# Joining the exit stage of a state space layer and the projection stage that follows it into one software pipeline

## The reference, cut to what matters

```python
y = y * rsqrt(mean(y*y) + 1e-5) * rms_w          # mamba2: gated output, root mean square norm
ym = y @ W_out + skip_scale * xs
ym = layernorm(ym, ln_w, ln_b)                   # over the 128 channels of a token
x = x + (ym @ proj_w + proj_b)
t = layernorm(x)                                 # over the channels, no weights
h = t @ W_gat                                    # 16 columns: 4 heads x 4 experts
a_src, a_dst = (h*att_src).sum(-1), (h*att_dst).sum(-1)      # 4 columns each
```

## Time and profile before

| | |
|---|---|
| median of 3 runs | 17695.13 us (17678.79 to 17721.8) |
| the profiled execution | 17696.22 us, its span 17694.7 us |
| `mamba_out` in the trace | from 11103 to about 11614 us |
| `heads`, second call | from about 11614 to 11976 us |
| busy share of the span | PE 41%, DVE 45%, ACT 25%, POOL 54% |

### The profile page before, as it was taken

How to read it: one execution, slowest core, us unless ns; L and a number is a source line. 1 busy time by engine, 2 the same in 40 slices (tenths; PEclk the granted TensorE clock), 3 DMA queues, 4 the chain that set the end, 5 groups by cost and what they waited for, 6 DMA issues and landing times. The chain is left out here.

```text
span 17694.7 us, 238235 instructions
## 1 busy us (share of the span) xinstructions
PE 7275.7 (41%) x86506; PEld 3912.4 (22%) x86506; DVE 7922.3 (45%) x12617; ACT 4414.1 (25%) x7103; POOL 9481.4 (54%) x10003
## 2 busy tenths in 40 slices
PE   0179711145221222136799999872112211222114
PEld 0123311023110111012355555331111111111012
DVE  9978576643111111175688888531111111111128
ACT  0123233322110011005665566641001110111000
POOL 0012477777777777660110000157777777777764
PEclk9589855577665666568899999986556655666556
DMA  1011221143222222244211111443222222222226
GB/s 47 0 50 44 72 52 21 20 114 113 61 61 55 54 61 62 57 156 131 60 49 48 46 48 49 154 119 65 58 55 58 61 58 55 58 61 61 53 55 224
DMA packets 949454, 1207.72 MB, mean 68 GB/s; under 512 B 371956, under 2 KB 587092, under 8 KB 929236
## 3 DMA queue, kind: packets, MB, share of 16 engines
q1 hardware_dynamic: 394036, 571.90, 9.9%
q0 software_dynamic: 328768, 179.97, 7.4%
q10 hardware_dynamic: 225888, 444.68, 7.4%
HBM read 672.45 MB, written 523.25 MB: 68 GB/s over the span
## 5 line engine op out<-in xcount | busy, mean ns | idle before, releaser
L1005 POOL DMA_INDIRECT g_got<-table,g_ring x8192 | 7740.1, 945 | 2520.4 <-issue 2490.9
L1203 DVE TENSOR_TENSOR g_z<-g_gs,g_wide 128x512 f32<-128x512 f32 x64 | 44.0, 688 | 5364.3 <-DMA g_gs<-rows 5364.3
L1046 PE MATMUL g_ffn<-g_xn,g_w 128*128 128x512 f32 x1024 | 556.9, 688 | 3967.1 <-ACT g_hid L1060 3940.4
L1046 PE MATMUL g0s_turn<-g_xn,g_w 128*128 128x512 f32 x1024 | 554.3, 685 | 2670.4 <-ACT g0s_ei L1060 2669.1
L1159 ACT ACTIVATE g_wide<-g_z 128x512 f32<-128x512 f32 x64 | 38.5, 601 | 6083.4 <-DVE g_z L1203 6083.4
L571 POOL DMA_INDIRECT m2b_got<-dst,k_blki x256 | 243.3, 950 | 2185.2 <-DVE m2b_le L583 2108.4
L1046 PEld LDWEIGHTS g_ffn<-g_xn,g_w 128*128 128x128 f32 x1024 | 190.4, 215 | 4287.6 <-ACT g_hid L1060 4193.6
L1046 PEld LDWEIGHTS g0s_turn<-g_xn,g_w 128*128 128x128 f32 x1024 | 189.7, 214 | 2988.8 <-ACT g0s_ei L1060 2921.7
L1338 POOL DMA_INDIRECT g_tot<-state,k_last_row x512 | 598.5, 1169 | 156.1 <-issue 156.1
L571 POOL DMA_INDIRECT cb_got<-dst,k_blki x256 | 250.6, 979 | 725.4 <-DVE cb_le L583 662.4
L951 POOL DMA_INDIRECT ad<-h_hs,k_start_row x512 | 504.5, 985 | 242.9 <-issue 147.7
(11 more groups left out here) (438 smaller groups left out, 19170.3 us busy)
## 6 DMA issues: line engine op xcount, KB each, us to landing
g_got<-table,g_ring POOLq DMA_INDIRECT x8192
ffn<-g_y ACTq DMA_DIRECT2D x128, 1024.0 KB
g_yin<-ffn SPq DMA_DIRECT2D x128, 1024.0 KB
rows<-g_got SPq DMA_DIRECT2D x512, 192.0 KB
g_gs<-rows ACTq DMA_DIRECT2D x64, 1536.0 KB, 6.4
state<-g_out ACTq DMA_DIRECT2D x64, 1536.0 KB, 5.5
h_x<-x SPq DMA_DIRECT2D x128, 256.0 KB
xn<-h_xn ACTq DMA_DIRECT2D x128, 256.0 KB
```

Of the source, the lines that this page charges most:

```text
L1005: pool.indirect_dma_start(self.got[:,par,k,:],None,self.table,bass.IndirectOffsetOnAxis(ap=self.ring[:,par,k:k+1].bitcast(u32),axis=0)).th ...
L1046: TE.matmul(self.hP[:,f,:],self.w1[:,e,f*P:f*P+P],self.xs[:,par,:],start=True,stop=True).then_inc(self.up,1)
```

## The change

The second call of `heads` goes, and its work becomes further sub-stages of `mamba_out`, on tiles that are still in SBUF: x3 is stored but not loaded again.

- PE gets `hn` mean (5), `hn` variance (6) and `table_rows` (7). Its order in a step is 6, 0, 5, 2, 3, 7, 4, 1.
- ACT gets `hn` square (6), `hn` root (7) and `leave` (8): a copy of the table rows out of PSUM, the store of xn, a second copy of the 16 a_dst columns into `adst`, and the store of the table rows. Its order is 7, 4, 1, 6, 3, 0, 8: the three roots, then the three squares, then `leave`. `root` has one Ln of 1024 columns in place of two of 512.
- DVE gets `hn` centre (5) and `hn` scale (6). Its order is 5, 2, 6, 3, 1, 4, 0.
- Both Norms share one variance bank, `vP`: nm's variance of tile i waits for hn's Ln of tile i-3, hn's variance of tile i for nm's Ln of tile i+2.
- `adst` has a place for each of the 64 tiles, so the scatters of POOL need no buffer back; POOL waits for them once at the end.
- Loading x and storing x3 move from POOL to SP, whose program is written out in full, without a loop: in step k y and xs of tile k, x of tile k-3, store of x3 of tile k-5.
- In every Norm of the program the logarithm is written over the squares (`self.log=self.sq`).

```diff
...
-    def __init__(self, nc, room, name, mean_w, eps, source, arrived, dest, dest_free):
+    def __init__(self, nc, room, name, mean_w, eps, source, arrived, dest, dest_free, var=None, var_free=None, mean=None):
...
-        self.log=room.sb(name+"_log",[P,2,T])
+        self.log=self.sq
...
-        self.mean=room.pb(name+"_mean",[P,T])
-        self.var=room.pb(name+"_var",[P,T])
+        self.mean=room.pb(name+"_mean",[P,T]) if mean is None else mean
+        self.var=room.pb(name+"_var",[P,T]) if var is None else var
+        self.var_free=var_free
...
+        if self.var_free: self.var_free(pe,i)
         self.nc.tensor.matmul(self.var[:,:],self.mean_w,self.sq[:,par,:],start=True,stop=True).then_inc(self.spread.sem,1)
...
         qP=r.pb("qP",[P,T])
+        vP=r.pb("vP",[P,T])
+        hp=r.pb("hp",[P,2,4,HW])
...
-        out=Stores(r,"out")
-        squared,meaned,logged,rooted,scaled,mixed,skipped,affine,projected,added=r.flags("squared meaned logged rooted scaled mixed skipped affine projected added")
-        nm=Norm(nc,r,"n",mw[:,:],eps[:,0:1],lambda i,par:ym[:,par,:],lambda e,i,par: skipped.of(e,i),lambda i,par:nn[:,par,:],lambda e,i,par: projected.before(e,i,2))
+        x_out_in,xn_stored,t_stored=r.pair("x_out"),r.pair("xn_out"),r.pair("t_out")
+        def stored(eng,sems,i,par):
+
+            if not (isinstance(i,int) and i<2): eng.wait_ge(sems[par],(i-par)*8)
+        sent=r.sem("sent")
+        picked=r.sem("picked")
+        send_gate=r.sem("send_gate")
+        squared,meaned,logged,rooted,scaled,mixed,skipped,affine,projected,added,rows,copied=r.flags("squared meaned logged rooted scaled mixed skipped affine projected added rows copied")
+        def rows_free(dve,i,par):
+            stored(dve,xn_stored,i,par)
+            rows.before(dve,i,2)
+        nm=Norm(nc,r,"n",mw[:,:],eps[:,0:1],lambda i,par:ym[:,par,:],lambda e,i,par: skipped.of(e,i),lambda i,par:nn[:,par,:],lambda e,i,par: projected.before(e,i,2),
+                vP[:,:],lambda e,i: hn.logged.of(e,i-3))
+        hn=Norm(nc,r,"hn",mw[:,:],eps[:,0:1],lambda i,par:xo[:,par,:],lambda e,i,par: added.of(e,i),lambda i,par:xn[:,par,:],rows_free,
+                vP[:,:],lambda e,i: nm.logged.of(e,min(i+2,TILES-1) if isinstance(i,int) else i+2))
...
+            for d,v in ((wos[:,:,:],wo),(rm[:,:],rms),(sk[:,:],skip.partition_broadcast(P)),(lw[:,:],lnw),(lb[:,:],lnb),(pws[:,:],pw),(pbs[:,:],pb),(sm[:,:],same_mean),(mw[:,:],ones),
+                        (w[:,0:16],wg),(at[:,:],att.partition_broadcast(P))):
+                sp.dma_start(d,v).then_inc(w_in,16)
+            def load(i):
+                scaled.before(sp,i,2)
+                sp.dma_start(yt[:,i%2,:,:],y.rearrange("q p n -> p q n")[:,:,i*T:(i+1)*T]).then_inc(y_in[i%2],16)
+                skipped.before(sp,i,2)
+                at_=i//TPI*PADT+i%TPI*T+2
+                sp.dma_start(xst[:,i%2,:],xs[:,at_:at_+T]).then_inc(s_in[i%2],16)
+            def load_x(i):
+                added.before(sp,i,2)
+                sp.dma_start(xt[:,i%2,:],x[:,i*T:(i+1)*T]).then_inc(x_in[i%2],16)
+            def store(i):
+                added.of(sp,i)
+                sp.dma_start(x_out[:,i*T:(i+1)*T],xo[:,i%2,:]).then_inc(x_out_in[i%2],16)
+            for k in range(TILES+5):
+                if k<TILES: load(k)
+                if 0<=k-3<TILES: load_x(k-3)
+                if k>=5: store(k-5)
+            for sems in (x_out_in,xn_stored,t_stored):
+                for v in sems: sp.wait_ge(v,TILES//2*16)
         @block.tensor
         def _(pe):
             nm.pe_start(pe)
-            for f in (meaned,mixed,projected): f.start(pe)
-            pe.wait_ge(w_in,16*9)
-            pe.wait_ge(ready,1)
+            hn.pe_start(pe)
+            for f in (meaned,mixed,projected,rows): f.start(pe)
+            pe.wait_ge(w_in,16*11)
+            pe.wait_ge(ready,3)
...
-            lagged(pe,TILES,[mean_square,mix,lambda i,p:nm.pe_mean(pe,i,p),lambda i,p:nm.pe_var(pe,i,p),project],last_first=True)
+            def table_rows(i,par):
+                hn.normed.of(pe,i)
+                copied.before(pe,i,1)
+                for q in range(4):
+                    last=nc.tensor.matmul(hp[:,par,q,:],xn[:,par,q*P:(q+1)*P],w[:,:],start=True,stop=True,skip_group_check=True)
+                last.then_inc(rows.sem,1)
+            lagged(pe,TILES,[mean_square,mix,lambda i,p:nm.pe_mean(pe,i,p),lambda i,p:nm.pe_var(pe,i,p),project,lambda i,p:hn.pe_mean(pe,i,p),lambda i,p:hn.pe_var(pe,i,p),table_rows],order=[6,0,5,2,3,7,4,1])
...
-                for q in range(2):
-                    last=nc.scalar.activation(rs[:,par,q,:],rP[:,q,:],ACT.Ln,bias=eps[:,0:1])
-                last.then_inc(logged.sem,1)
+                nc.scalar.activation(rs[:,par,:,:],rP[:,:,:],ACT.Ln,bias=eps[:,0:1]).then_inc(logged.sem,1)
                 logged.of(act,i)
                 nc.scalar.activation(rs[:,par,:,:],rs[:,par,:,:],ACT.Exp,scale=-0.5).then_inc(rooted.sem,1)
-            lagged(act,TILES,[square,root,lambda i,p:None,lambda i,p:nm.act_square(act,i,p),lambda i,p:nm.act_root(act,i,p)],last_first=True)
+            def leave(i,par):
+                rows.of(act,i)
+                stored(act,t_stored,i,par)
+                nc.scalar.copy(hs[:,par,:,:],hp[:,par,:,:]).then_inc(copied.sem,1)
+                nc.scalar.dma_start(xn_out[:,bass.ds(i*T,T)],xn[:,par,:]).then_inc(xn_stored[par],16)
+                copied.of(act,i)
+                nc.scalar.copy(adst[:,bass.ds(i,1),:,:].rearrange("p a q f -> p (a q) f"),hs[:,par,:,20:24]).then_inc(picked,1)
+                nc.scalar.dma_start(table[bass.ds(i*T,T),:].rearrange("(q p) f -> p q f",p=P),hs[:,par,:,:]).then_inc(t_stored[par],16)
+            lagged(act,TILES,[square,root,lambda i,p:None,lambda i,p:nm.act_square(act,i,p),lambda i,p:nm.act_root(act,i,p),lambda i,p:None,
+                              lambda i,p:hn.act_square(act,i,p),lambda i,p:hn.act_root(act,i,p),leave],order=[7,4,1,6,3,0,8])
...
+            for k in range(2):
+                nc.vector.tensor_tensor(prod[:,k,:],w[:,0:16],at[:,16*k:16*k+16],ALU.mult).then_inc(w_prod,1)
+            dve.wait_ge(w_prod,2)
+            for k in range(2):
+                nc.vector.tensor_reduce(w[:,16+4*k:20+4*k],prod[:,k,:].rearrange("p (h e) -> p h e",e=4),AX.X,ALU.add).then_inc(ready,1)
...
             def add_x(i,par):
                 projected.of(dve,i)
                 landed(dve,x_in,i,par)
-                out.done.before(dve,i,2)
+                stored(dve,x_out_in,i,par)
+                hn.centred.before(dve,i,2)
                 nc.vector.scalar_tensor_tensor(xo[:,par,:],qP[:,:],pbs[:,0:1],xt[:,par,:],ALU.add,ALU.add).then_inc(added.sem,1)
-            lagged(dve,TILES,[scale,add_skip,lambda i,p:nm.dve_centre(dve,i,p),norm,add_x],last_first=True)
+            lagged(dve,TILES,[scale,add_skip,lambda i,p:nm.dve_centre(dve,i,p),norm,add_x,lambda i,p:hn.dve_centre(dve,i,p),lambda i,p:hn.dve_scale(dve,i,p)],order=[5,2,6,3,1,4,0])
         @block.gpsimd
         def _(pool):
-            load(1,1)
-            with pool.Fori(0,TILES//2-1) as t:
-                for par in range(2):
-                    store(t*2+par,par)
-                    load(t*2+par+2,par)
-                    out.landed(pool,t*2+par,par)
...
+            for i in range(TILES):
+                pool.wait_ge(picked,i+1)
+                pool.sem_inc(send_gate,1)
+                for q in range(4):
+                    k=i*4+q
+                    pool.indirect_dma_start(ad,bass.IndirectOffsetOnAxis(ap=keep.start_row[:,k:k+1],axis=0),adst[:,i,q,:],None).then_inc(sent,16)
+            pool.wait_ge(sent,TILES*64)
...
-        mamba_out(nc,y,xs,x2,a["wo"],a["rms"],a["skip"],a["lnw"],a["lnb"],a["pw"],a["pb"],a["c_same_mean"],a["c_ones"],x3)
-        project(1,x3)
+        mamba_out(nc,y,xs,x2,a["wo"],a["rms"],a["skip"],a["lnw"],a["lnb"],a["pw"],a["pb"],a["c_same_mean"],a["c_ones"],x3,
+                  a["wg1"],a["att1"],xn,table,keep[1],ad[1])
         attend(1,x3,out)
```

More of the change, by code:

```diff
@@ L2083, with mamba_out @@
 PADT=TOK+2
-def mamba_out(nc, y, xs, x, wo, rms, skip, lnw, lnb, pw, pb, same_mean, ones, x_out, tag="m3"):
+def mamba_out(nc, y, xs, x, wo, rms, skip, lnw, lnb, pw, pb, same_mean, ones, x_out, wg, att, xn_out, table, keep, ad, tag="m3"):
     with ExitStack() as ctx:
@@ L2097, in mamba_out @@
         xo=r.sb("xo",[P,2,T])
+        xn=r.sb("xn",[P,2,T])
+        hs=r.sb("hs",[P,2,4,HW])
+        adst=r.sb("adst",[P,TILES,4,4])
         wos=r.sb("wo",[P,2,P])
@@ L2106, in mamba_out @@
         mw=r.sb("mw",[P,P])
+        w=r.sb("w",[P,HW])
+        at=r.sb("att",[P,32])
+        prod=r.sb("prod",[P,2,16])
         eps=r.sb("eps",[P,1])
@@ L2158, in _ @@
             nm.act_start(act)
-            for f in (squared,logged,rooted): f.start(act)
-            act.wait_ge(ready,1)
+            hn.act_start(act)
+            for f in (squared,logged,rooted,copied): f.start(act)
+            act.wait_ge(ready,3)
             def square(i,par):
```

(16 more changed lines are left out.)

4 lines of the change are left out of this document (3 added, 1 removed).

## The result

| | before | after |
|---|---|---|
| median | 17697.57 us (4 runs, 17678.79 to 17721.8) | 17539.82 us (4 runs, 17508.98 to 17553.2) |
| the profiled execution | 17696.22 us, span 17694.7 | 17508.98 us, span 17507.3 |
| the two stages, first instruction to that of the next stage | 872.8 us | 699.9 us |

A forecast was written before the change was run, and what follows sets the result against it. It took chains of waits (exit stage) and POOL's scatters with SP's order (projection) as bounds, no engine full. Start, 63 steps and tail put the next stage at 11797 against 11975.9, 179 us less: 17517 us, range 17465 to 17600.

The forecast's parts named there:

- The step, 10.23: Joined stage: a ring of waits from one hn square to the next through ACT and PE, 10.23 us a tile.
- A: Favoured case: the ring of 10.2 us sets the joined stage's step, kernel at 17517 us; chance 0.77.
- PE's sum, 8.7: Joined stage: PE's own work for one tile, 8.7 us; no step can be shorter.
- The cover of `leave`, 2.3: Joined stage, ACT: 2.3 us of spare time before the nm root hides `leave` and the hn root.
- the shared bank, 1.8: Joined stage: hn's Ln frees the variance bank at 3.9, nm variance wants it at 5.71; 1.8 us spare.
- New waits on transfers, nothing: Joined stage: DVE's wait for xn's landing and SP's loads of y stay hidden, costing nothing.
- The start: Fill of the joined stage: first square at 11112.6, then eight steps of 69.8 us together.
- Rival D: Joined stage: TensorE's clock falls, steps up to 17.3 us, kernel up to 17971 us; chance 0.07.
- 55 steps: Joined stage after the first eight steps: 55 steps of 10.23 us, 562.6 us.
- The tail, 52: Joined stage, 64th square to the next stage: 52 us, with a bound of 10 either way.
- B: Rival: PE's work sets the joined stage's step at 8.7 us, kernel at 17422 us; chance 0.04.
- C: Rival: `leave` or a landing outlasts its cover, steps of 11.5 us, kernel at 17599 us; chance 0.12.

The follow-up runs named there:

- run 1: Changed kernel with PE's nm variance moved from fifth to third in its order, ahead of both means; 17413.92 us, ratio 0.9849 to the kernel before.
- run 5: Changed kernel with six more 512-column squares on ACT in each `leave`, their result unread; 17582.77 us.
- run 8: Changed kernel with each tile of y loaded a second time by SP into a buffer nobody reads; 17477.17 us.
- run 2: Changed kernel with ACT's three squares ahead of its three roots; 17943.6 us.
- Run 7: Changed kernel without three of the four a_dst scatters of each tile; 17494.11 us.
- Run 3: Kernel with ACT's squares first (run 2), plus ten unread products of 256 columns in PE's pause behind the nm mean; 17718.15 us.

## Why the prediction held, point by point

- **The step, 10.23.** Measured 10.15. Link by link from the hn square at 11397.26 to the next at 11407.41, in the forecast's order, with its value behind each: hn square to square of y 1.04 (1.08), square 1.17 (1.09), mean_square 1.82 (1.82), hn mean 0.85 (0.86), nm mean 0.86 (0.86), nm variance to its Ln 1.06 (1.19), Ln to Exp 0.72 (0.70), to `root` 0.54 (0.54), joined Ln 1.12 (1.13), Exp to the hn square 0.97 (0.96). The sum is 10.15 (10.23). Two links were off by more than 0.04: I had the variance 0.13 too long, with 0.17 behind its 1.02 from the earlier trace rows where it was 0.04, and the square 0.08 too short. In the next step they are 1.14 and 1.09, and the sum is 10.15 again. It came out as a ring, and run 1 shows that it was the limit and not merely a sum that fits. What I gave for A, that the same reckoning gives 7.54 where the trace has 7.54, was no test: starts read from one mix to the next add up to that step whatever holds it. The old steps also alternate between 7.41 and 7.54, 7.47 in the mean. The forecast of the new step did not rest on it.
- **PE's sum, 8.7.** Run 1 gives 8.62 with PE full.
- **The cover of `leave`, 2.3, and the shared bank, 1.8.** ACT's wait for the nm variance is 2.3 in the mean, and run 5 gives 2.5 to the first cost. I named the nm root as what comes late next; it is the bank, whose spare time is 2.1 (hn's Ln over at 11400.91, the nm variance at 11403.00).
- **New waits on transfers, nothing.** No wait of PE, DVE or ACT for a load or a landing shows in the middle, and run 8 moved 33% more bytes without a longer step there. The y load had less spare time than I reckoned only under run 2's order.
- **The start.** The first square comes 9.5 us into the stage, as forecast. The first eight steps took 72.1, not 69.8. The first four were 1.9 shorter than forecast, the other four 4.2 longer. The rows at 11132.46 and 11144.10 show why: mean_square stood 3.28 and 2.42 us for a square and then took 3.78 and 2.69 where 1.98 is usual at full clock. With the two products behind each, that is some 4.8 us, my estimate from the rows. The two steps there took 11.65 and 11.77. Rival D was real in the fill, for 2 of 64 tiles.
- **55 steps.** 558.3, not 562.6.
- **The tail, 52.** Measured 60.0, the one term that was mis-sized by more than a few us, though within its bound of 10. Up to the last copy of a_dst it was 42.0 us where I had 41. I put four scatters, 5 us, behind that copy; the last one started 12.3 behind it. In the last five steps of the drain the copies come 2.6 to 4.9 us apart, less than the 5.1 us that a tile's scatters take, so POOL fell nearly two tiles behind while I reckoned it as idle. Run 7 gives back 8.4 us by leaving out three scatters of four.
- **The sum.** 9.5 + 72.1 + 558.3 + 60.0 = 699.9, against 9.5 + 69.8 + 562.6 + 52 = 693.9. The step's 4 us too much and the start's and tail's 10 too little partly cancel. The remaining 4.8 us behind the stage and 9.7 ahead of it I had at 0; none of the runs explains them, and their sign changes from run to run. That the profiled execution is only 8 us from 17517 is therefore partly luck: 14.5 us that I had not forecast outweigh the 6.0 that the stage is longer than reckoned.
- **The rivals.** B is not the change but what run 1 makes of it. C is refuted in both its forms (runs 1, 5, 8). D does not happen in the middle at pauses of 0.25 to 0.83 us and does in run 2 at 4.4 to 5.6 us. The rule of the Trainium skill that I weighed for it ("TensorE: Matmul & The Clock Gate", section "A second HAM failure mode: psum-queue depth-cycling") has TensorE pause often between matmul groups that go round the banks, and its clock swing with that. Here the banks and their number are the same in the kernel after and in run 2, and the granted clock is 1.00 in the one, with two short pauses in every step, and 0.80 in the other, with one long one. Run 3, with the same banks and the pause filled, is back at 1.00. In these runs the clock goes with the length of the pause, not with the banks and not with the number of pauses.
- **What the change's name credits.** Joining itself brings the gain: the projection stage's 361.6 us go, and the steps grow by 2.7 us over 64 tiles. Roots ahead of squares is worth much (run 2, 404 us of stage, of which run 3 gives back 168.5 with the clock), centring first 11.5 us, the joined Ln 9 to 11 on the old stage, all a_dst in SBUF nothing. The shared variance bank and SP's part in place of POOL's were not tested by runs.

## What to carry to other kernels

Write a software pipeline's step down as a ring: follow from one instruction to its next appearance each wait and each place in a queue, and add up start to start. If the ring is longer than the fullest engine's sum, look for the instruction on it that stands in its queue behind others nobody waits for, and move it ahead: here that brought 93 us for one product. Reckon the drain by itself, for an engine with time to spare in a full step can be the slowest in a short one.

## What the runs showed of the hardware that I had not expected

- ScalarE's issue of a DMA can run ahead of its arithmetic. In the kernel after, the store of xn (L2219) is issued at 11406.92, while the copy that stands before it in the program (L2218) runs at 11409.39, 2.5 us later. The issue of the table rows (L2222) does not: it waits for the copy, stands at 11399.72 for 0.39 us, and ACT has 0.43 us of idle time with only "issue" behind it before the hn Ln at 11400.22. Over the steps from 11200 to 11700 that idle time is 0.6 us in the mean, near the 0.5 that I had put down to the two issues together; the cover hides it.
- A pause of TensorE of 3.28 us was followed by records at half clock (3.78 for four), and one of 2.42 us by records partly at half clock (2.69), while pauses of up to 0.83 in every step of the middle left the granted clock at 1.00.
- Work that nobody needs can pay: 4.5 us of products in a pause shortened a 17.1 us step to 13.9, with the granted clock at 1.00 where it had been 0.80.
